# Two transformer-like layers on one core: routed results of the second layer scattered by block instead of gathered by tile

## What is computed

```
x = x + attention(layernorm(x)) * silu(ffn(layernorm(x)))
```

```
w, idx = top_k(router(x), 4)                     # 4 experts of 16 for each token
y[t]   = sum over k of w[t,k] * expert[idx[t,k]](x[t])
z      = shared expert(x)                        # inner size 352, an expert's is 176
ffn    = y + z
```

## Time and profile before

| what | us |
|---|---|
| median of 3 runs (1879.03, 1892.84, 1884.45) | 1884.45 |
| the profiled execution | 1877.61 |
| its span, first to last instruction | 1875.8 |
| PE busy | 1759.5 (94%) |
| DVE busy | 1271.0 (68%) |
| ACT busy | 895.3 (48%) |
| POOL busy | 857.1 (46%) |

### The profile page before, as it was taken

One profiled execution on the slowest core, in us unless ns is written; L12 is line 12 of the kernel. 1 busy time (PEld: TensorE's weight loads), 2 busy tenths in 40 slices (PEclk: granted clock), 3 DMA queues, 4 the chain that ended last, 5 costly groups with the idle time before them and its releaser, 6 DMA issues.

```text
span 1875.8 us, 34780 instructions
## 1 busy us (share of the span) xinstructions
PE 1759.5 (94%) x11726; PEld 1432.7 (76%) x11726; DVE 1271.0 (68%) x2787; ACT 895.3 (48%) x2954; POOL 857.1 (46%) x943
## 2 busy tenths in 40 slices
PE   5999998899989999999999999999999998999875
PEld 4666666677878887888888888888888876777765
DVE  4888898644687888876766667666676653444466
ACT  3767776543234444444544544545545433444211
POOL 2011014200666655657677677676676760000255
PEclk8999999999989999999999999999999999999977
DMA  7964643242420000000000000000001233333333
GB/s 237 300 227 143 209 130 112 77 148 88 167 93 1 1 12 1 7 1 15 21 15 15 20 15 22 15 13 23 12 23 57 79 115 106 108 106 107 99 109 112
DMA packets 104684, 148.26 MB, mean 79 GB/s; under 512 B 11888, under 2 KB 84720, under 8 KB 102096
## 3 DMA queue, kind: packets, MB, share of 16 engines
q1 hardware_dynamic: 95168, 119.95, 19.8%
q0 software_dynamic: 9216, 25.18, 4.0%
q10 hardware_dynamic: 144, 1.05, 0.1%
HBM read 81.64 MB, written 64.49 MB: 78 GB/s over the span
## 4 chain that ended last, share of the span: by engine, by line
PE 80%; DVE 9%; issue 3%; DMA 2%; ACT 2%; POOL 2%; another core or an unknown queue 1%; SPq 0%; POOLq 0%; DVEq 0%; ACTq 0%
PE ps L1424 12%; PE ps L1439 9%; PE ps L1511 5%; PE ps L1958 5%; PE ps L1465 4%; PE ps L705 4%; PE ps L1453 3%; PE ps L1452 3%; PE ps L1451 3%; PE ps L959 2%; PE ps L1446 2%; PE ps L1975 2%; PE ps L724 2%; PE ps L1977 2%; PE ps L695 2%
## 5 line engine op out<-in xcount | busy, mean ns | idle before, releaser
L1424 PE MATMUL ps<-work,weights 128*128 128x256 f32 x1024 | 248.0, 385 | 1.2 <-DVE work L1697 1.2
L1439 PE MATMUL ps<-split 128*128 128x512 f32 x768 | 227.9, 419 | 0.0
L1424 PEld LDWEIGHTS ps<-work,weights 128*128 128x128 f32 x1024 | 185.6, 190 | 23.8 <-DVE work L1697 1.6
L1839 POOL TENSOR_TENSOR work<-work,rope 128x512 f32<-128x512 f32 x128 | 164.8, 1288 | 52.8 <-ACT work L1612 52.8
L2158 POOL DMA_INDIRECT work<-yg,work x64 | 63.2, 988 | 245.6 <-DMA yg<-work 208.5
L1845 POOL TENSOR_TENSOR work<-work 128x512 f32<-128x512 f32 x128 | 164.5, 1285 | 5.0
L1439 PEld LDWEIGHTS ps<-split 128*128 128x128 f32 x768 | 130.8, 190 | 24.8
L827 DVE COPY work<-ps 128x384 f32<-128x384 f32 x256 | 130.1, 551 | 19.8 <-PE ps L705 19.4
L810 ACT ACTIVATE work<-ps,work 128x128 f32<-128x128 f32 x256 | 94.7, 370 | 86.0 <-DVE work L907 73.9
L705 PE MATMUL ps<-ident,work 128*128 128x128 f32 x768 | 115.9, 283 | 17.7 <-DVE work L827 15.8
L1511 PE MATMUL ps<-weights,work 128*128 128x256 f32 x512 | 124.7, 388 | 2.5 <-ACT work L1668 2.5
(11 more groups left out here) (242 smaller groups left out, 4410.2 us busy)
## 6 DMA issues: line engine op xcount, KB each, us to landing
heads_by_part<-split SPq DMA_DIRECT2D x64, 256.0 KB, 3.9
split<-heads_by_part SPq DMA_DIRECT2D x64, 256.0 KB
work<-xg SPq DMA_DIRECT2D x118, 128.0 KB
yg<-work SPq DMA_DIRECT2D x118, 128.0 KB, 1.7
xg<-work SPq DMA_DIRECT2D x13, 1024.0 KB, 5.9
weights<-in_w SPq DMA_DIRECT2D x8, 1024.0 KB, 6.2
weights<-in_f SPq DMA_DIRECT2D x8, 1024.0 KB, 5.1
weights<-in_f SPq DMA_DIRECT2D x8, 608.0 KB, 4.9
```

Of the source, the lines that this page charges most:

```text
L1424: last = pe.matmul(ps[:, 2, which * SEQ:(which + 1) * SEQ], w1(h, (which * KC + kc) * P, P), xT[:, kc, :], start=kc == 0, stop=kc == KC - 1)
L1439: last = pe.matmul(ps[:, 3, :], x1_split[:, xp, kc, c * P:(c + 1) * P], w_vg[:, n % 2, wp, kc, :], start=i == 0, stop=i == KC * len(TERMS) ...
L1839: pool.tensor_tensor(qk[:, h % 4, :, :], raw[:, h % 2, :, :], rope[:, 0, :].unsqueeze(1).broadcast_to([P, 2, SEQ]), ALU.mult).then_inc(rot ...
```

## The change

Six things change:

- Each block's result is now scattered from SBUF straight to places by token, in the new DRAM tensor `yk1`: row k*2048 + token holds that token's result of choice k, and padding rows go to rows of their own behind. POOL does it, one indirect DMA of 128 rows for each block, 79 in all, at most three in flight. SP's store of the block goes away. The ring `y4` has 36 buffers instead of 3.
- For this the places have to be known by block. POOL scatters the token numbers (64 indirect DMAs of 128 numbers of 4 bytes, `give_id`) into the DRAM tensor `ids1`: 32 of them beside the sequences 2 to 7, in the pairs that had one scatter so far, and 32 after the attention. SP clears `ids1` first and loads it back at block 22; PE turns it at block 26, ACT copies it, POOL makes integers of it. Only then does POOL begin with the scatters.
- In the tile loop, POOL fetches a tile's four routed rows with one plain DMA of 512 KB instead of four gathers. It begins when all scatters have landed.
- SP's wait and store of the output lag four tiles behind its loads.
- PE's sequences 2 to 5 become a loop with two sequences in its body, run twice.
- One more constant of 32 KB is loaded at the start.

```
+BEHIND_OUT = 4
+RINGY1 = 12 * RINGY
...
-        yg1 = nc.dram_tensor("yg1", (NB1 * P, D), F32, kind="Internal").ap()
+        ids1 = nc.dram_tensor("ids1", (NB1 * P, 1), F32, kind="Internal").ap()
+        yk1 = nc.dram_tensor("yk1", (K1 * TOK + NB1 * P, D), F32, kind="Internal").ap()
...
+        y4 = carve("experts", RINGY1, D)
+        IDS_AT = 22
+        IDS_EARLY = 2 * (BATCH - 2) * PAIR1 - TILES * K1
...
+                if n == IDS_AT + RINGX:
+                    pe.wait_ge(ids_loaded.sem, ids_loaded.at(0, 16))
+                    last = pe.transpose(ps[:, n % 2, D:D + NB1], ids_rows, ident[0:NB1, 0:NB1])
+                if n == IDS_AT + RINGX:
+                    act.copy(ids_f, ps[:, n % 2, D:D + NB1]).then_inc(ids_copied.sem, 1)
-                if b >= RINGY:
-                    act.wait_ge(y4_stored[b % RINGY].sem, y4_stored[b % RINGY].at(0, 16 * (b // RINGY)))
+                if b >= RINGY1:
+                    act.wait_ge(y4_spread[b % RINGY].sem, y4_spread[b % RINGY].at(0, 16 * ((b - RINGY1) // RINGY + 1)))
...
+        def give_id(pool, n):
+            c, k = n // K1, n % K1
+            pool.indirect_dma_start(out=ids1[:, :], out_offset=bass.IndirectOffsetOnAxis(ap=route1.index[:, k, c:c + 1], axis=0),
+                                    in_=token_row[:, n:n + 1], in_offset=None).then_inc(route1.scattered.sem, 16)
         def pool_blocks1(pool):
             def fetch(c):
                 if c >= 2:
                     pool.wait_ge(z4_ready.sem, z4_ready.at(0, c - 1))
-                for k in range(K1):
-                    pool.indirect_dma_start(out=yk4[:, c % 2, k, :], out_offset=None, in_=yg1[:, :],
-                                            in_offset=bass.IndirectOffsetOnAxis(ap=route1.index[:, k, c:c + 1], axis=0))\
-                        .then_inc(yk4_loaded[c % 2].sem, 16)
+                pool.dma_start(yk4[:, c % 2, :, :], yk1[0:K1 * TOK, :].rearrange("(k c p) d -> c p k d", k=K1, p=P)[c])\
+                    .then_inc(yk4_loaded[c % 2].sem, 16)
+            for n in range(IDS_EARLY, TILES * K1):
+                give_id(pool, n)
+            pool.wait_ge(ids_copied.sem, ids_copied.at(0, 1))
+            pool.tensor_copy(ids_i, ids_f).then_inc(ids_ready.sem, 1)
+            pool.wait_ge(ids_ready.sem, ids_ready.at(0, 1))
+            for b in range(NB1):
+                pool.wait_ge(y4_copied.sem, y4_copied.at(0, b + 1))
+                if b >= RINGY:
+                    pool.wait_ge(y4_spread[b % RINGY].sem, y4_spread[b % RINGY].at(0, 16 * (b // RINGY)))
+                pool.indirect_dma_start(out=yk1[:, :], out_offset=bass.IndirectOffsetOnAxis(ap=ids_i[:, b:b + 1], axis=0),
+                                        in_=y4[:, b % RINGY1, :], in_offset=None).then_inc(y4_spread[b % RINGY].sem, 16)
...
-                if b >= 2:
-                    store_block(b - 2)
+                if b == IDS_AT:
+                    sp.wait_ge(route1.scattered.sem, route1.scattered.at(0, route1.at_all()))
+                    sp.dma_start(ids_rows, ids1.rearrange("(b p) o -> b (p o)", p=P)).then_inc(ids_loaded.sem, 16)
-            for c in range(TILES):
+            for c in range(TILES + BEHIND_OUT):
                 if NB1 + c + RINGX < UNITS1:
                     load_block(NB1 + c + RINGX)
-                if c % 2:
-                    sp.wait_ge(x2_ready.sem, x2_ready.at(0, c + 1))
-                    sp.dma_start(x_out[:, c - 1:c + 1, :], x_res[:, c - 1:c + 1, :]).then_inc(stored, 16)
+                n = c - BEHIND_OUT
+                if n > 0 and n % 2:
+                    sp.wait_ge(x2_ready.sem, x2_ready.at(0, n + 1))
+                    sp.dma_start(x_out[:, n - 1:n + 1, :], x_res[:, n - 1:n + 1, :]).then_inc(stored, 16)
...
+                    if len(here) == 1:
+                        give_id(pool, 2 * at - here[0])
-            for t in range(2, SEQ_END):
+            with pe.Fori(2, SEQ_END - 1, 2) as t:
                 pe_slots(pe, t, "middle")
+                pe_slots(pe, t + 1, "middle")
+            pe_slots(pe, SEQ_END - 1, "middle")
```

More of the change, by code:

```diff
@@ L147, in build @@
         g_half = sb("g_half", [P, 1])
+        token_row = sb("token_row", [P, TILES * K1])
         LEFT = (nc.sbuf_bytes_remaining // 4) - 8
@@ L1912, in build @@
         xb4T = carve("experts", 2, D)
-        y4 = carve("experts", RINGY, D)
         h4 = carve("experts", 2, 2 * P)
@@ L1923, in build @@
         UNITS1 = NB1 + TILES
+        ids_rows = carve("experts", P, parts=NB1)
+        ids_f, ids_i = carve("experts", NB1), carve("experts", NB1, dt=mybir.dt.int32)
+        IDS_AT = 22
+        IDS_EARLY = 2 * (BATCH - 2) * PAIR1 - TILES * K1
         F1_PARTS = PAIR1 + (E1 * EW - W1O + 2 * D - 1) // (2 * D)
@@ L1936, in build @@
             again(n, TILES) for n in (z_ready, out_th_ready, z_gated, z_mixed, x1_ready))
+        ids_cleared, ids_loaded, ids_copied = again(x_first, 16), again(x_loaded, 16), again(w0_loaded, 16)
+        ids_ready = again(w0_loaded, 17)
+        y4_spread = [again(xs_scattered[n], 16 * K1 * TILES // RINGS) for n in range(RINGY)]
         h4_cleared, z4_step, sh1_loaded = again(h_cleared, 1), again(z_step, 0), again(f0_loaded, 16 * (E0 + 1))
@@ L2051, in copy_y @@
                 act.wait_ge(y4_done.sem, y4_done.at(0, b + 1))
-                if b >= RINGY:
-                    act.wait_ge(y4_stored[b % RINGY].sem, y4_stored[b % RINGY].at(0, 16 * (b // RINGY)))
-                act.copy(y4[:, b % RINGY, :], ps[:, 6 + b % 2, 0:D]).then_inc(y4_copied.sem, 1)
+                if b >= RINGY1:
+                    act.wait_ge(y4_spread[b % RINGY].sem, y4_spread[b % RINGY].at(0, 16 * ((b - RINGY1) // RINGY + 1)))
+                act.copy(y4[:, b % RINGY1, :], ps[:, 6 + b % 2, 0:D]).then_inc(y4_copied.sem, 1)
             def out_tanh(c):
@@ L2110, in combine @@
                 dve.wait_ge(y4_done.sem, y4_done.at(0, n + 1))
-                dve.wait_ge(yk4_loaded[c % 2].sem, yk4_loaded[c % 2].at(0, 16 * K1 * (c // 2 + 1)))
+                dve.wait_ge(yk4_loaded[c % 2].sem, yk4_loaded[c % 2].at(0, 16 * (c // 2 + 1)))
                 dve.scalar_tensor_tensor(z, yk4[:, c % 2, 0, :], route1.coef[:, 0, c:c + 1], ps[:, 6 + n % 2, 0:D],
@@ L2156, in fetch @@
                     pool.wait_ge(z4_ready.sem, z4_ready.at(0, c - 1))
-                for k in range(K1):
-                    pool.indirect_dma_start(out=yk4[:, c % 2, k, :], out_offset=None, in_=yg1[:, :],
-                                            in_offset=bass.IndirectOffsetOnAxis(ap=route1.index[:, k, c:c + 1], axis=0))\
-                        .then_inc(yk4_loaded[c % 2].sem, 16)
+                pool.dma_start(yk4[:, c % 2, :, :], yk1[0:K1 * TOK, :].rearrange("(k c p) d -> c p k d", k=K1, p=P)[c])\
[11 more added lines that the diff above has]
+                                        in_=y4[:, b % RINGY1, :], in_offset=None).then_inc(y4_spread[b % RINGY].sem, 16)
             for n in range(RINGY):
-                pool.wait_ge(y4_stored[n].sem, y4_stored[n].at(0, 16 * len(range(n, NB1, RINGY))))
+                pool.wait_ge(y4_spread[n].sem, y4_spread[n].at(0, 16 * len(range(n, NB1, RINGY))))
             for c in range(TILES):
@@ L2170, in build @@
                        (lower0, "lower0"), (lower1, "lower1"), (router1, "router1"), (rope, "rope"),
-                       (keep_a, "keep_a"), (keep_w, "keep_w"), (s1w, "s1w"),
+                       (token_row, "token_row"), (keep_a, "keep_a"), (keep_w, "keep_w"), (s1w, "s1w"),
                        (weights[0:RS, W0S:W0S + NH1 * M], "s2w")]
@@ L2258, in _ @@
                     load_pair(0)
+                    sp.dma_start(ids1.rearrange("(b p) o -> b (p o)", p=P), A["no_row"]).then_inc(ids_cleared.sem, 16)
             def load_block(b):
@@ L2375, in beside @@
                     if t == SCATTER_FROM and pp == 1:
+                        pool.wait_ge(ids_cleared.sem, ids_cleared.at(0, 16))
                         pool.wait_ge(route1.slots_ready.sem, route1.slots_ready.at(0, 1))
                     at, pairs = (t - SCATTER_FROM) * PAIR1 + pp - 1, (BATCH - SCATTER_FROM) * PAIR1
-                    for n in range(at * TILES * K1 // pairs, (at + 1) * TILES * K1 // pairs):
+                    here = range(at * TILES * K1 // pairs, (at + 1) * TILES * K1 // pairs)
+                    if len(here) == 1:
+                        give_id(pool, 2 * at - here[0])
+                    for n in here:
                         c, k = n // K1, n % K1
@@ L2532, in _constants @@
         "ident": np.eye(P, dtype=np.float32),
+        "token_row": (np.arange(K1)[None, None, :] * TOK + np.arange(TILES)[None, :, None] * P + p[:, None, None])
+        .reshape(P, TILES * K1).astype(np.float32),
+        "no_row": (K1 * TOK + np.arange(NB1 * P)).astype(np.float32).reshape(NB1, P),
         "causal": bias,
```

5 lines of the change are left out of this document (removed).

## The result

The changed kernel took 1915.87 us (median of 4 runs, 1913.28 to 1928.87), the kernel before 1882.38 beside it: a ratio of 1.0194, interval 1.0166 to 1.0223. I had forecast 1848 and given "slower" 0.11. The profiled execution took 1913.28 us, its span 1911.5, for 1875.8: 35.7 us more, where 32.5 less were expected.

The account below looks back on a forecast made before the run. PE was taken to bound nearly everything, with gain only in the last stage: 1875.8 - 36.5 + 4.0 = 1843.3, with 1.8 between span and execution 1845, up to 1852 by the median's offset; forecast 1848 us, range 1834 to 1874.

Parts of the forecast that it names:

- slower: The case that the changed kernel takes above 1903.3 us; chance 0.11.
- Last stage: Final tile loop: one plain fetch replaces four gathers, SP's loads run ahead, DVE sets the pace; -36.5 us.
- Block scatters: Block loop: numbers come in time and POOL's scatters of block results stay hidden behind PE; cost 0.
- the run that catches up: Block loop: POOL starts with 23 blocks waiting, catches up in 63 us at 1.3 us each; cost 0.
- Rival 1: Block loop: long runs of POOL's DMAs hold up PE's signals, 61 us for 111 DMAs, 1909 us; chance 0.12.
- Numbers beside the attention: Attention pairs with one scatter get a second indirect DMA, hidden by POOL's idle time; cost 0.
- PE's loop: Attention: one jump back over a two-sequence body costs a code packet and a landing; +4.0 us.
- registers: PE's loop: 640 waits on register values, taken as hidden, 0; as a rival, +29 us to 1877, chance 0.05.
- SP's wait at block 22: Block loop: numbers out by 1600, asked for at 1617.5, needed three blocks later; no delay, cost 0.
- The cover I had named: Block loop: numbers ready before SP asks, PE needing them three blocks later, only later block loads behind SP's wait.

Follow-up runs that it names:

- e5: The kernel before with only SP's last-stage waits and stores lagging four tiles, gathers kept; 1856.01 us, ratio 1.0005.
- e12: The kernel before with 32 extra scatters of 1 KB rows at the block loop's start, POOL pausing after every fourth, run again; 1856.41 us, ratio 1.0007.
- e10: The changed kernel once more, on a quick chip; 1882.27 us against 1854.70 for the kernel before, ratio 1.0150.
- e6: The changed kernel with all 64 number scatters beside the attention, still asked for at block 22; 1857.64 us, ratio 1.0010.
- e16: The changed kernel with all number scatters beside the attention, asked for at block 0, and PE's loop undone; 1854.81 us, ratio 0.9994.
- e18: As e16, but numbers 64 bytes apart, each scatter writing 64 bytes a row, result ring 12 deep; 1868.94 us, ratio 1.0074.
- e17: The changed kernel with numbers 64 bytes apart, each scatter writing 64 bytes a row, result ring 30 deep; 1863.96 us, ratio 1.0039.
- e9: The changed kernel with POOL pausing after every fourth DMA of both runs, numbers asked for at block 24, PE's loop undone; 1956.47 us, ratio 1.0556.
- e8: The kernel before with 32 extra scatters of 1 KB rows at the block loop's start, POOL pausing after every fourth; 1857.36 us, ratio 1.0004.
- e2: The kernel before with 32 extra unbroken indirect scatters of 1 KB rows at the block loop's start; 1913.80 us, ratio 1.0162.
- e3: The kernel before with 32 extra plain DMAs of 128 KB from POOL's queue at the block loop's start; 1890.86 us, ratio 1.0049.
- e15: The kernel before with 32 extra scatters of 64 bytes a row, side by side, at the block loop's start; 1857.09 us, ratio 1.0013.
- e13: The kernel before with 32 extra scatters of 4-byte rows 1 KB apart at the block loop's start; 1858.06 us, ratio 1.0017.

## Why the prediction was wrong, point by point

- **Last stage**, -36.5: right in kind and in size, -35.4 measured (122.4 to 87.0). DVE's 4.14 a tile, POOL under 1 us a tile, SP ahead: as written. The 1.1 us missing lie in the start: the first fetch goes at 1839.27, 14.8 us after block 77 starts, for 13.7 in my sum (1767.1 - 1753.4); the last block's result is copied late and its scatter lands only after. On a quick chip the gathers cost before less (106.0 and 107.2 us with no late signal in e5 and e12), and the gain is about 20 (107.2 to 87.2). So that the size came out is partly the luck of the chip. SP's lag alone counts nothing there (e5).
- **Block scatters**, 0: the step that failed first. "32 scatters at 1.3 are out by 1600" was right to 5 us (1604.4), and POOL's time was all it priced. It never asked what they do to the DMA engines that SP's loads of x share. Written side by side in 4-byte rows they cost 37.7 us: 32.4 in blocks 1 to 8 and 5.3 before block 0 (34.1 and 7.6 in e10). From this alone the sign is turned.
- The same step, **the run that catches up**, 0: on the slow kind 27.5 us for some 28 scatters. Where I wrote "against: scatters write to DRAM" the trace offered no run of scatters, and I took the absence for evidence. On a quick chip this step was right: 0 (e6, e10).
- **Rival 1** had 61 us and 1909; 60.0 us in the block loop and 5.3 before it were measured, and 1913.28 for the profiled execution. The price is right half by accident: its mechanism, late signals in a run of POOL's DMAs, is that of the second stop alone, at 0.98 us a DMA instead of 0.55. The first has another mechanism, which no rival named: it stands on quick chips too, with no late signal in it. 0.12 was too little for a rule that the earlier trace rows bore out four times in four.
- **Numbers beside the attention**, 0: right on a quick chip (e10: sequences of 121.1, as in e12), about 0.5 to 1 us a sequence on the slow one, in pairs of 15.1 that were 14.9. Scattered by ones, the neighbouring rows do no harm there; by ones and twos they do some (e16 against e18, 123.0 to 124.6 us a sequence against 121.8 to 123.0).
- **PE's loop**, +4.0: the pair at the jump takes 19.4 instead of 15.1 (4.3), 2.8 with the loop alone, 4.9 in e10 and 5.7 in e17; registers 0. Right. In the changed kernel PE stands there 2.60 us with nothing to wait for, which it doesn't in the kernel before:

```profile
1084.52 1.65 PE L1469 MATMUL ps<-work 64*128 64x256 f32 x16 [2.60 <-issue]
```

  The Trainium skill's "Runtime: NRT & Kernel Launch" (Instruction fetch mechanics) has a rule for such a stop, the fetch of the code jumped to; these traces agree with it, but that it is the fetch, no run shows.
- **SP's wait at block 22**, 0: right; in e9 PE waited 53.4 us for the same numbers, when they were late. The cover I had named was the right thing to name.
- The sum put right for this chip: -35.4 + 4.3 + 37.7 + 27.5 + 1.4 (rest of the attention) = +35.5; measured +35.7.

**Open.** Why one chip and the kernels shown before have late signals and three chips haven't; whether it is the chip or its condition. Whether gaps in a run prevent them there (e8, e12 fell on quick chips), and what e2 itself, without pauses, does on a quick one. How much of it is the indirect form (e3 is shorter, too). How near rows must be to do harm: between 4 and 64 bytes nothing was tried, nor 4-byte rows 64 bytes apart, nor what in the memory it is. What the change is worth without any stop: no run has it.

## What to carry to other kernels

A DMA hidden by time on its queue may still take the engines that a critical load needs: ask of each new one not only when it is issued, but how it writes. Don't scatter 4-byte rows side by side beside a critical load: rows of 64 bytes (e15), or 4-byte rows 1 KB apart (e13), cost next to nothing. A load with 79 rows outermost runs on one DMA engine of 16. And before believing a cost of a few per cent, run it on a second chip: here one of the two stops, and nearly half of the gain, belonged to the chip.

## What the runs showed that I had not expected

- 32 scatters of 128 rows, 4 bytes side by side: 45.8 us; the same 1 KB apart: 2.9.
- The kernel before itself takes 1882 us on one chip and 1855 on three, some 15 of the 27 us in its last stage (122.4 us from block 77, against 107.2 in e12, which leaves that stage alone), where the gathers' run is.
- 32 unbroken indirect DMAs of 1 KB rows stop PE, ACT and DVE for 32.5 us on one chip (e2); on another 32 of 64-byte rows cost 1.9 us (e15), and 64 unbroken gathers of 1 KB rows make no signal late there (e5).
- A load of 79 rows of 8 KB: one packet every 0.31 us, 24.5 us in all.
